# Edge projection one turn later in the first layer of a two-layer graph network

## What is computed

```python
rel_t = last_update[src] - t
rel_t_enc = jnp.cos(rel_t[:, None] * time_w[None, :] + time_b)
edge_attr = jnp.concatenate([rel_t_enc, msg], axis=-1)       # 32 + 64
e = (edge_attr @ We).reshape(-1, HEADS, CH)                  # edge projection
k = k_all[src] + e
alpha = jnp.sum(q_all[dst] * k, axis=-1) / math.sqrt(CH)
a = softmax of alpha over the edges of one target
out = segment_sum((v_all[src] + e) * a, dst) + x @ Wskip + bskip
x = layernorm(x + out)                                       # layer 0
agg = segment_sum(vals[:, None] * x[cols], rows)             # layer 1
x = layernorm(x + agg @ W.T + b)
```

## Time and profile before

| what | value |
|---|---|
| plain runs, median of three | 10764.61 us |
| profiled execution, span (first to last instruction) | 12598.2 us |
| busy: PE, DVE, POOL, ACT | 71%, 67%, 59%, 35% |
| mean granted clock of TensorE (1 is 2.4 GHz, 0.5 is 1.2 GHz) | 0.736 |
| first layer's loop in the profiled execution | about 330 to 6450 us |
| second layer's loop | about 6600 to 12500 us |

### The profile page before, as it was taken

How to read it: one execution, slowest core, us unless ns; L and a number is a source line. 1 busy time by engine, 2 the same in 40 slices (tenths; PEclk the granted TensorE clock), 3 DMA queues, 4 the chain that set the end, 5 groups by cost and what they waited for, 6 DMA issues and landing times. The chain is left out here.

```text
span 12598.2 us, 265221 instructions
## 1 busy us (share of the span) xinstructions
PE 8900.6 (71%) x52864; PEld 8210.4 (65%) x52865; DVE 8472.5 (67%) x20487; ACT 4468.2 (35%) x18126; POOL 7477.0 (59%) x7644
## 2 busy tenths in 40 slices
PE   5577776777777776677646666777777787877755
PEld 2566666666666666666645656777777777777744
DVE  6677777777777677777784444666666666666656
ACT  1344444444444444444433333222222222222200
POOL 0666666666666666666636666666666666666620
PEclk7777878777777778878765555677777777777788
DMA  5555555555555555555532221344444444444433
GB/s 150 139 143 144 145 147 143 144 146 146 143 144 146 142 144 146 144 145 144 145 78 59 58 58 57 102 114 111 111 111 111 111 114 111 113 113 110 112 106 96
DMA packets 1646739, 1526.64 MB, mean 121 GB/s; under 512 B 796583, under 2 KB 1367619, under 8 KB 1646499
## 3 DMA queue, kind: packets, MB, share of 16 engines
q1 hardware_dynamic: 1374244, 848.34, 26.6%
q0 software_dynamic: 272384, 677.07, 19.1%
HBM read 1269.62 MB, written 254.87 MB: 121 GB/s over the span
## 5 line engine op out<-in xcount | busy, mean ns | idle before, releaser
L785 POOL DMA_INDIRECT kv<-kv_scratch,arena x3520 | 3545.0, 1007 | 2394.7 <-issue 1412.7
L834 POOL DMA_INDIRECT message_scratch<-ohT,idx x3232 | 3489.7, 1080 | 2063.9 <-issue 1356.1
L1035 PE MATMUL bank<-oh,kve 128*128 128x128 f32 x8640 | 1746.4, 369 | 818.0 <-DVE arena L1764 663.3
L1035 PEld LDWEIGHTS bank<-oh,kve 128*128 128x128 f32 x8640 | 1554.3, 266 | 982.2 <-DVE arena L1764 763.9
L1104 ACT ACTIVATE arena<-arena,weights 128x65 f32<-128x65 f32 x7040 | 1771.6, 337 | 3.0 <-PE bank L943 2.5
L1006 PE MATMUL bank<-ones,featT 98*128 98x1 f32 x6464 | 1191.0, 305 | 791.8 <-ACT kv L1187 473.5
L1006 PEld LDWEIGHTS bank<-ones,featT 98*128 98x128 f32 x6464 | 1177.1, 272 | 842.9 <-issue 777.8
L1453 DVE TENSOR_TENSOR arena<-kv,bank 128x512 f32<-128x512 f32 x880 | 599.5, 681 | 1587.6 <-remote 1513.5
L1111 ACT ACTIVATE featT<-bank 96x512 f32<-96x512 f32 x880 | 520.0, 591 | 2798.2 <-remote 1504.9
L943 PE MATMUL bank<-arena,oh 128*128 128x130 f32 x7040 | 1289.8, 342 | 231.4 <-issue 128.8
L934 PE MATMUL bank<-arena,ohT 128*128 128x128 f32 x7040 | 1266.1, 330 | 216.0 <-issue 214.7
(11 more groups left out here) (220 smaller groups left out, 12442.7 us busy)
## 6 DMA issues: line engine op xcount, KB each, us to landing
kve<-message_scratch SPq DMA_DIRECT2D x2160, 129.0 KB
kve<-nodes_scratch SPq DMA_DIRECT2D x880, 256.0 KB
feat<-in_edge_attr_dram SPq DMA_DIRECT2D x880, 96.0 KB
feat<-block_scratch SPq DMA_DIRECT2D x812, 98.0 KB
kv<-kv_scratch,arena POOLq DMA_INDIRECT x3520
arena<-q_scratch SPq DMA_DIRECT2D x880, 64.0 KB
message_scratch<-ohT,idx POOLq DMA_INDIRECT x3232
feat<-in_edge_attr_dram SPq DMA_DIRECT2D x880, 32.0 KB
```

The costliest lines, as they stand in the source:

```text
L785: pool.indirect_dma_start(kv[:, k, g, :], None, kv_d, bass.IndirectOffsetOnAxis(ap=took[:, j, g, 0:1].bitcast(I32), axis=0)).then_inc(s_ga ...
L834: pool.indirect_dma_start(msg_d, bass.IndirectOffsetOnAxis(ap=idx[:, k, g:g + 1], axis=0), sum_ring[:, k % RING1, g, :], None).then_inc(s_ ...
L1035: op = pe.matmul(banks[SEG_BANKS[sg.slot(BR)]][:, 0:P], mt[:, sg.slot(MT), a, 0:C], seg_oh[:, sg.slot(MT), a, :], start=(a == 0), stop=(a ...
```

## The change

PE's edge projection (`e_stage`) is called with 14 ahead in place of 15. So it works on the step whose transposition PE made in its turn before, where it worked on the step transposed in the same turn. DVE's two additions (`ve_stage`, `ke_stage`) are called with 13 in place of 14. The place of the three in their engine's turn is the same, and nothing else is changed.

```diff
                 for k in range(UNROLL0):
                     if first_of(k, 5, ROUND):
                         at(i, k, (alphaT_stage, 5))
-                    at(i, k, (feat_stage, 15), (sum_stage, 1), (q_stage, 14), (e_stage, 15))
+                    at(i, k, (feat_stage, 15), (sum_stage, 1), (q_stage, 14), (e_stage, 14))
...
-                    at(i, k, *turn[0], (ve_stage, 14), *turn[1], (ke_stage, 14), *turn[2], (block_stage, 0), *once(5, forward_stage),
+                    at(i, k, *turn[0], (ve_stage, 13), *turn[1], (ke_stage, 13), *turn[2], (block_stage, 0), *once(5, forward_stage),
                        (onehotT_stage, 15), *once(5, backward_stage), (product_stage, 13), *once(4, run_stage, first_stage),
```

## The result

The changed kernel takes 10851.53 us (median of 4 runs, 10848.51 to 10856.0) against 10769.32 us for the kernel before (4 runs, 10761.37 to 10785.85): 82 us slower, ratio 1.0072 with a 95% interval of 1.0058 to 1.0086. The forecast was 10763, the range ended at 10850.

The account below looks back on a forecast made before the run. It took POOL's own work, 5.5 us a step, to bound the first layer's loop in plain runs. Every term was priced 0, so 10764.6 + 0 against the median; forecast 10763 us, range 10635 to 10850.

Parts of the forecast that it names:

- What bounds the kernel: First layer's loop: without recording stalls POOL's own work sets the pace, 5.5 us a step, DVE close behind, PE third.
- recording holds the engines up: Profiled span: 12598.2 us against a plain median of 10764.61, 1834 us more, taken as stalls caused by recording.
- Rival B: PE, not POOL, closes the turn, so a projection that needn't wait shortens it: 10635 or 10504 us; chance 25%.
- PE's projection, 0: PE's projection a turn later: its 260.9 us wait for ACT's copy goes, part moving to the transposition; 0 at POOL's pace.
- DVE's additions, 0: DVE's additions of V and K a turn later: still need a projection from PE's turn before, release unchanged; 0.
- The ring: POOL's ring of eight gathers: slots held a turn longer, slack falling from 15.5 to 10 us, still above zero; 0.
- Rival C: The ring runs dry: gathers wait for K's addition, 1.9 us in each of 55 loop passes, 103 us, 10868; chance 17%.
- The product q·k now reads a K that DVE wrote in the same turn: DVE's product depends on its own turn's K, with the one-hot between: taken as 0, at most 35 us.
- POOL's 1.25 us per issue: POOL's two-step work: eight gather issues starting 1.25 us apart, then two short operations, 10.97 us in all.
- The clock: TensorE's half or full clock: removing a PE wait could pay twice, but PE's idle time per step stays; not counted.

Follow-up runs that it names:

- z_k_late: Kernel before with K's addition alone moved by a turn, its product following in the same turn; V's addition and PE's projection unmoved: 10856.19 us.
- z_dve_only: Kernel before with DVE's additions of V and K moved by a turn, PE's projection left in the turn of its transposition: 10852.67 us.
- y_selfwait: Kernel before with nothing moved, only the product's wait for a K added in the same DVE turn put in: 10848.52 us.
- y_took_early: Changed kernel with the eight waits of the once-a-round rel0 subtraction put ahead of the product, every operation in place: 10774.51 us.

## Why the prediction was wrong

- *What bounds the kernel: right, for a wrong reason.* That "in plain runs the first layer goes at POOL's pace" holds: DVE waits for POOL 440 times of 440. The estimate of 5.5 us a step was 5.75. But "recording holds the engines up" was wrong. Spans without the stalls (10771.4 and 10849.8) equal plain times within 3 us, and plain runs with them take 12598.59.
- *Rival B, PE's turn:* it did not happen. The section of the Trainium skill cited there judges TensorE by its share of the peak rate and by its weight loads, not by the busy time of its products; by weight loads PE had 66% in the earlier trace rows (3896.98 of 5900 us), next to POOL's 65%. Neither order finds the pace: in the changed kernel's loop DVE is the busiest (85%), and POOL (79%) sets it.
- *PE's projection, 0:* right. Its wait for the copy was 0.7 us where POOL sets the pace, and PE waits of 400 us (z_k_late, z_dve_only) cost nothing either. That part of the wait would move to the transposition was not seen (0.8 us).
- *DVE's additions, 0:* right as to the moves. V's wait for PE fell from 56.2 to 29.4 us.
- *The ring, price 0:* right, slack from 15.56 to 10.06 us where 15.5 and 10 were given. Rival C did not happen, although the time landed near its 10868: by its sign (the time rises and the gathers wait longer) it could have been taken for right, but the gathers wait for no K, they last longer.
- *"The product q·k now reads a K that DVE wrote in the same turn ... Bounds: 0, and 0.04 x 880 = 35 us ... I take 0": this is the step that failed.* It took the new wait at 0 because it asked only how long the product itself would stand, and that is indeed nothing: DVE's operations start at the same distances. It left out what is queued behind the waiting instruction. The wait stops the sequencer from running ahead, so that eight later waits are passed 1.4 us later against the gather. Then a gather that had started just before the one-hot and taken no notice of it is held to its end, once a round, 0.65 us. That is 71 us of the 82 directly, and y_selfwait shows that the wait alone gives all of it (10848.52). y_took_early keeps the wait and takes the eight others from behind it, and nothing is left of the loss (10774.51). Why the passing of eight waits decides the close call stays open.
- *Above that, POOL's 1.25 us per issue was taken as a constant.* The three issues of the earlier trace rows take 0.99, 0.95 and 0.95; others of the loop take up to 1.9, and I had not looked at their spread. By the holds counted above, one-hot 0.76, angles 0.76, scan 0.94, `new` and L1503 0.27 us a round, 2.7 us of 46 are holds, 0.34 us a step. An engine that sets the pace and whose instructions vary in length has a second bound beside its own work, and none of my rivals was about it. I had argued that POOL paces and then priced DVE's edits by DVE's time alone.
- *The clock:* 0.790 and 0.792 on average, no part in it.

## What to carry to other kernels

When GpSimd issues gathers back to back and sets the pace, price an edit on VectorE by which of its two-operand operations will run beside the start of a gather, not by VectorE's own time; and read the gathers' durations by their place in the loop before trusting one of them. A wait that delays its own operation by nothing can still cost: it takes away the sequencer's lead, so list every wait behind it. A saving at one gather moves all the following ones and is easily handed back at the next two-operand operation; test the neighbouring orders instead of one.

## What was not expected of the hardware

- Two kernels with VectorE and GpSimd operations at equal distances (0.09 to 0.10 us) differ by 0.65 us in a gather's issue, in all of 80 rounds. They differ in whether eight other waits stand ahead of one semaphore wait or behind it (y_took_early and the changed kernel).
- An issue that finds VectorE in a two-operand operation is longer by its rest, 0.279 us for 0.282 on average, and by two back to back 0.93; a small GpSimd subtraction went from 0.22 to 0.93 us beside a scan.
- The scan forward held gathers for 0.94 us in one order, for nothing in another and for 0.107 us, nearly its rest, in a third. What decides it is open.
